# Two slots of scores and four banks of value sums in an attention stage whose ScalarE hardly rests

## The chip, the cores and the metric

The kernel runs on one core of one Trainium2 chip. The metric is the device time of one execution in microseconds (us); lower is better. A core has the matrix engine TensorE (PE), the vector engine VectorE (DVE), ScalarE (ACT), GpSimd (POOL) and the queue engine SyncE (SP). Each runs its own program in order, and they wait for one another through counting semaphores. Matmuls write to PSUM, which holds 8 banks of 512 fp32 values for each of its 128 partitions.

## The reference, cut to what matters

Input x is 2 sequences of 1024 tokens with 128 channels. Four layers follow one another, `x = x + layer(layernorm(x))`, in the order A (a gated recurrence), F, B (a Fourier layer), F. The change lies in layer F, which is run twice with the same weights:

```python
h = _rms(x, n1_w)
q = _rms(heads(wq), qn_w); k = _rms(heads(wk), kn_w); v = heads(wv)   # 16 heads of 8 channels
scores = einsum('bhqd,bhkd->bhqk', q, k) * HD ** (-0.5)
scores = where(causal, scores, -inf)
attn = softmax(scores)
ao = einsum('bhqk,bhkd->bhqd', attn, v) @ wo.T
x = x + ao                      # then a mixture of four small expert networks
```

The reference calls the layer with T = 1024 tokens and B = 2 sequences, so the attention is causal over 1024 x 1024 for 32 pairs of sequence and head.

## The kernel before, in words

Attention in `hybrid_kernel` is a list of units, `ATT` (L1129 to L1131). The outer index `it` is an item: one of the 2 sequences and one of 4 groups of four heads, 8 items in a layer. Inside an item the queries are taken in two chunks of 512 (`qc` 0 and 1), the keys in tiles of 128 (`kt` 0 to 3 for `qc` 0, and 0 to 7 for `qc` 1). On the diagonal the columns left of `c0` are skipped. A unit is one slot of scores and one exponential. Where c0 is 0 or 128, a key tile is two units of two heads each; where c0 is 256 or 384, one unit has all four heads. So an item has 20 units, here called u0 to u19:

- `qc` 0: u0, u1 (kt 0, 512 columns), u2, u3 (kt 1, 384 columns), u4 (kt 2, 256), u5 (kt 3, 128).
- `qc` 1: u6 to u15 (kt 0 to 4, two units each, 512 columns), u16, u17 (kt 5, 384), u18 (kt 6, 256), u19 (kt 7, 128).

In elements of a partition, an exponential is 1024 wide in fourteen units (512 columns by two heads, or 256 by four), 768 in u2, u3, u16 and u17, and 512 in u5 and u19. Sixteen items, or 320 units, are worked through in the whole kernel.

Four engines share the work of a unit u:

- PE in `f_tensor`, the loop of L1258: the scores S(u), matmuls of L1271 (bf16), into the slot `u % DEPTH` of two banks. Ahead of them stands `wait_ge(probs_ready, rep * NA + u + 1)` (L1265). ACT raises this semaphore by DEPTH at the start (L1390) and by one with every exponential, so S(u) waits for the exponential of unit u - DEPTH. Behind S(u) in the same loop, PE works on the unit w = u - 4 (`LAG`), if w ends a key tile: the value sums V(w), matmuls of L1289 (fp32), four heads beside one another in four strips of 32 rows of one bank. V(w) waits for the exponential of w (L1280), for its mask if it lies on the diagonal (L1282), and at kt 0 for `o_read` (L1284), that is, until DVE has read the sums that this bank held before.
- ACT in `f_scalar` (L1438 to L1445): the exponential X(u), from the slot into one of six buffers `PX` (PDEPTH).
- POOL in `f_gpsimd` (L1217 to L1224): the mask of the twelve units of an item that lie on the diagonal (u0 to u5, u14 to u19), a multiplication in PX. Ahead of u4 it also copies the values of the next item (L1211).
- DVE in `f_vector` (L1542 to L1561): when the last key tile of a chunk is summed, it reads the bank twice, with a shuffle (L1552) and, after a reciprocal (L1554), with a multiplication (L1556), which sets `o_read`; then it adds into `AO` (L1560).

The eight banks are split 6 to 2: slots of scores in banks 0 to 5, value sums in banks 6 and 7, one for each `qc`. What PE does in order around the change is thus ... S(15), V(11), S(16), S(17), V(13), S(18), S(19), V(15), then of the next item S(0), S(1), V(17), S(2), V(18), S(3), V(19), S(4), S(5), V(1), S(6), S(7), V(3), S(8), V(4), S(9), V(5), S(10), S(11), V(7) ... A V in the first half of this list is one of the item before.

After attention come the output projection and the experts, which use the banks anew; they wait for all of the above.

Of the kernel before, what the change touches and what calls it, by code (L numbers as in the profile page):

```python
# [27 lines left out]
CH = 512  # L28
# [64 lines left out]
def hybrid_kernel(nc, x, a_w, a_wab, a_small, a_conv, a_bog, a_bout, a_wout, b_w, b_dft, b_idft,  # L93
                  f_w, f_n, f_qk, f_mid, f_down, f_wo, f_rows, eye, causal, out):
    ctx = ExitStack()
    with ctx:
# [3 lines left out]
        def sb(name, shape, dt=F32, at=None, side=None):  # L100
            return (at or ctx).enter_context(nc.sbuf_tensor(name, shape, dt, side=side))
# [16 lines left out]
        PS = ctx.enter_context(nc.psum_tensor("PS", [P, 8, CH], F32))  # L118
# [85 lines left out]
        with ExitStack() as sw:  # L204
# [15 lines left out]
            VA = [sb(f"VA{i}", [P, TB, GH, 32], at=sw) for i in range(2)]  # L220
# [166 lines left out]
        def dve_norm(v, link, ans, eps, dst, rms_eps=None):  # L387

            v.tensor_scalar(stat[:], mv[:, :, 1], eps, None, ALU.add).then_inc(to_act, 1)  # L389
            ans.wait()  # L390
            link(v.reciprocal(rstd[:], stat[:]))
            scale = rstd
            if rms_eps is not None:

                link(v.tensor_tensor(var[:], mv[:, :, 1], rstd[:], ALU.mult))
                link(v.tensor_tensor(var[:], var[:], rstd[:], ALU.mult))
                v.tensor_scalar(stat[:], var[:], rms_eps, None, ALU.add).then_inc(to_act, 1)
                ans.wait()
                link(v.reciprocal(rrms[:], stat[:]))
                link(v.tensor_tensor(rrms[:], rrms[:], rstd[:], ALU.mult))  # L400
                scale = rrms
            for b in range(B):
                for t in range(b * TB, (b + 1) * TB):
                    last = center_and_scale(v, dst, t, scale)
                last.then_inc(normed, 1)
# [13 lines left out]
        def act_sqrt(act, ask, ap):  # L419
            ask.wait()  # L420
            act.activation(ap, ap, ACT.Sqrt).then_inc(to_dve, 1)  # L421
# [714 lines left out]
        NA_Q0 = len([a for a in ATT if a[0] == 0 and a[1] == 0])  # L1136
        TILE_END = [u for u in range(NA) if ATT[u][3][-1] == GH - 1]
        LAG = 4
        DEPTH = 3
        OBANKS = 2  # L1140
        SCORES_BANKS = 2 * DEPTH
        ROUTER_BANK = 5
        HT_BANKS = 4
# [46 lines left out]
        def f_gpsimd(pool, link, nth, rep):  # L1190
# [15 lines left out]
            def values(it):  # L1206
                b, g = divmod(it, NG)
                if it >= 2:
                    pool.wait_ge(probs_used, PDEPTH + (rep * B * NG + it - 1) * NA_B)
                src = QKV[:, b * TB:(b + 1) * TB, 2 * D + g * (GH * HD):2 * D + (g + 1) * (GH * HD)]  # L1210
                pool.tensor_copy(VA[it % 2][:, :, :, HD * g:HD * (g + 1)],  # L1211
                                 src.rearrange("p t (h d) -> p t h d", d=HD)).then_inc(v_ready, 1)
# [4 lines left out]
            for u in DIAG:  # L1217
                it, qc, kt, heads, c0 = ATT[u]
                if it >= 1 and it + 1 < B * NG and (qc, kt, heads[0]) == (0, 2, 0):
                    values(it + 1)  # L1220
                pool.wait_ge(probs_ready, DEPTH + rep * NA + u + 1)
                halves = len(heads) // 2
# [3 lines left out]
        def f_tensor(pe, banks, nth, rep):  # L1226
# [11 lines left out]
            for b in range(B):  # L1238
# [4 lines left out]
                for c in chunks:  # L1243
                    for n in range(2):
                        k = banks.take()
                        for i in range(TPC):
                            last = pe.transpose(PS[:, k, i * P:(i + 1) * P], QKS[:, c * TPC + i, n * D:(n + 1) * D],
                                                ident[:])
                        last.then_inc(psum_full, 1)
                pe.wait_ge(shifts_ready, rep * B + b + 1)  # L1250
                for c in chunks:
                    k = banks.take()
                    for i in range(TPC):
                        last = pe.transpose(PS[0:H, k, i * P:(i + 1) * P], qst2[:, c * TPC + i, 0:H], ident[:])
# [3 lines left out]
            for u in range(NA + LAG):  # L1258
                if u < NA:
                    it, qc, kt, heads, c0 = ATT[u]  # L1260
                    b = it % 2
                    if u % NA_B == 0:
                        pe.wait_ge(stack_loaded[b], 64 * (rep * NG + it // 2 + 1))
                        pe.wait_ge(v_ready, rep * B * NG + it + 1)
                    pe.wait_ge(probs_ready, rep * NA + u + 1)  # L1265
                    for two in range(0, len(heads), 2):
                        at = two // 2 * (CH // 2)
                        for side in range(2):
                            rows = slice(SIDE * side, SIDE * (side + 1))
                            pair = heads[two] // 2  # L1270
                            last = pe.matmul(PS[:, 2 * (u % DEPTH) + side, at:at + CH - c0],  # L1271
                                             KS[b][rows, pair, kt * P:(kt + 1) * P],
                                             QS[b][rows, pair, qc * CH + c0:(qc + 1) * CH], start=True, stop=True)
                    last.then_inc(scores_ready, 1)
                if u - LAG in TILE_END:
                    w = u - LAG
                    it, qc, kt, heads, c0 = ATT[w]
                    b = it % 2
                    units = GH // len(heads)
                    pe.wait_ge(probs_ready, DEPTH + rep * NA + w + 1)  # L1280
                    if w in DIAG:
                        pe.wait_ge(probs_masked, rep * len(DIAG) + DIAG_DONE[w])  # L1282
                    if kt == 0:
                        pe.wait_ge(o_read, (rep * B * NG + it) * 2 + qc + 1)  # L1284
                    for h in range(GH):
                        px = PX[(w - (units - 1) + h // len(heads)) % PDEPTH]
                        i = h % len(heads)
                        at = i // 2 * (CH // 2)
                        last = pe.matmul(PS[32 * h:32 * h + 32, SCORES_BANKS + qc, c0:CH], VA[b][:, kt, h, :],  # L1289
                                         px[:, i % 2, at:at + CH - c0], start=(kt == 0),  # L1290
                                         stop=(kt >= TPC * qc), skip_group_check=True)
                    last.then_inc(probs_used, units)

            for c in range(NCH):
                if c % (NCH // B) == 0:
                    pe.wait_ge(heads_added, (rep * B + c // (NCH // B) + 1) * (NG - 1) * 2)
                for i in range(TPC):
                    t = (c * TPC + i) * P
                    last = pe.matmul(PS[:, c, i * OUTC:(i + 1) * OUTC], AO[:, t:t + P], fwo[:], start=True, stop=True)
# [17 lines left out]
            for t in range(TILES):  # L1317
                last = pe.matmul(PS[:, ROUTER_BANK, t * E4:(t + 1) * E4], HT[:, t * P:(t + 1) * P],
                                 fw[:, F_GATE:F_GATE + E4], start=True, stop=True)
# [68 lines left out]
        def f_scalar(act, link, ask, reads, nth, rep):  # L1388
            if rep == 0:
                act.sem_inc(probs_ready, DEPTH)  # L1390
            act_sqrt(act, ask, stat[:])
# [46 lines left out]
            for u in range(NA):  # L1438
                heads, c0 = ATT[u][3:]
                halves = len(heads) // 2  # L1440
                tile = lambda t: t.rearrange("p k (n q) -> p k n q", n=halves)[:, :, :, 0:CH - c0]
                k = 2 * (u % DEPTH)
                act.wait_ge(scores_ready, rep * NA + u + 1)
# [31 lines left out]
        def f_vector(v, link, ans, nth, rep):  # L1475
            base = FIRST_RESULT[nth]
            v.wait_ge(x_ready, nth)
            if rep == 0:
                v.sem_inc(o_read, OBANKS)
            dve_norm(v, link, ans, LN_EPS, SQ, F_EPS)  # L1480
# [61 lines left out]
            for it in range(B * NG):  # L1542
                b, g = divmod(it, NG)
                for qc in range(2):
                    at = (rep * B * NG + it) * 2 + qc
                    o = PS[:, SCORES_BANKS + qc, :]
                    t = b * S + qc * CH
                    v.wait_ge(probs_used, PDEPTH + (rep * B * NG + it) * NA_B + (NA_Q0 if qc == 0 else NA_B))
                    v.wait_ge(o_read, OBANKS + at)
                    if added:  # L1550
                        v.wait_ge(heads_added, added)
                    v.stream_shuffle(DEN[:], o, [HD * (g + 1) % 32] * 32).then_inc(den_ready, 1)  # L1552
                    v.wait_ge(den_ready, 2 * at + 1)
                    v.reciprocal(DEN[:], DEN[:]).then_inc(den_ready, 1)  # L1554
                    v.wait_ge(den_ready, 2 * at + 2)
                    v.scalar_tensor_tensor(out=DEN[:] if g else AO[:, t:t + CH], in0=o, scalar=frows[:, g:g + 1],  # L1556
                                           in1=DEN[:], op0=ALU.mult, op1=ALU.mult).then_inc(o_read, 1)
                    if g:
                        v.wait_ge(o_read, OBANKS + at + 1)
                        v.tensor_tensor(AO[:, t:t + CH], AO[:, t:t + CH], DEN[:], ALU.add).then_inc(heads_added, 1)  # L1560
                        added += 1  # L1561
# [102 lines left out]
        @block.tensor  # L1664
        def _(pe):
            banks = Banks(pe)
            for n, layer in enumerate(LAYERS):
                if layer == "A":
                    a_tensor(pe, banks)
                elif layer == "B":  # L1670
                    b_tensor(pe, banks, n)
                else:
                    f_tensor(pe, banks, n, LAYERS[:n].count("F"))
# [105 lines left out]
```

## Time and profile before

| | us |
|---|---|
| median of 3 runs | 1206.76 |
| lowest and highest run | 1203.33, 1211.42 |
| the profiled execution, its own time | 1207.07 |
| its span in the profile | 1205.2 |

The profile holds one execution. Times are us from the start of its span, unless they are marked ns. PE is the matmuls and PEld the loads of weights beside them. A row of a timeline gives start, length, engine, line, operation and shapes, how many instructions are merged in it, and in brackets how long the engine sat idle before it and what ended that. Instructions of a pipelined engine overlap, so the length of one is more than the distance between two. A wait for several semaphores is put down to the engine that came last by the profile, and this may be the wrong one. PEclk is the granted TensorE clock as a share of 2.4 GHz.

### The profile page before, as it was taken

The numbers are of one execution on the slowest core, as the hardware profiler recorded it, in microseconds if no ns is written. First come the engines' busy times: TensorE is split into PE (matmuls) and PEld (weight loads), VectorE is DVE, ScalarE is ACT, GpSimd is POOL, SyncE is SP. The second block draws the span as 40 slices with busy tenths as digits, with TensorE's granted clock in tenths as the row PEclk, the third lists the DMA queues.
The fourth block names the chain that finished last, engine by engine and source line by source line (L and its number), as shares of the span: only waits on it lengthen the run. The fifth ranks groups of instructions, "written<-read, shape, count | busy, mean of one in ns | idle before, by whom it ended". The sixth has DMA issues, their size and how long they took to land.

```text
span 1205.2 us, 11485 instructions
## 1 busy us (share of the span) xinstructions
PE 674.5 (56%) x4014; PEld 333.1 (28%) x4014; DVE 867.5 (72%) x1306; ACT 506.5 (42%) x752; POOL 403.4 (33%) x334
## 2 busy tenths in 40 slices
PE   4990000040004004479899799963264799978997
PEld 2450000040004003222222556631243122225655
DVE  6899999999999995856657733269959557667212
ACT  3423000122220001579999322243034899973321
POOL 1250847600006602226765000006802566650000
PEclk9985555555555556779999799987565899997999
DMA  2250006172000020223310000000003242100001
GB/s 92 70 140 1 1 0 140 35 168 63 13 14 14 0 35 0 84 75 116 97 33 22 1 1 1 1 0 1 0 0 115 63 142 54 54 1 1 1 1 35
DMA packets 30258, 50.71 MB, mean 42 GB/s; under 512 B 4472, under 2 KB 14328, under 8 KB 29176
## 3 DMA queue, kind: packets, MB, share of 16 engines
q1 hardware_dynamic: 29432, 49.32, 15.2%
q10 hardware_dynamic: 768, 0.66, 0.3%
q8 instruction: 32, 0.52, 0.2%
q14 instruction: 26, 0.21, 0.1%
HBM read 20.98 MB, written 16.92 MB: 31 GB/s over the span
## 4 chain that ended last, share of the span: by engine, by line
DVE 47%; PE 23%; ACT 16%; issue 10%; POOL 1%; DMA 1%; ACTq 1%; POOLq 0%; SPq 0%; DVEq 0%
ACT PX L1445 10%; PE PS L1330 6%; PE PS L1308 5%; PE PS L1350 4%; PE PS L1289 3%; DVE D L813 2%; DVE S L817 2%; DVE P L814 2%; DVE PS L871 2%; DVE PRD L870 2%; DVE mag L1031 2%; DVE PA L772 2%; ACT P L688 2%; DVE RO L837 2%; DVE RP L832 2%
## 5 line engine op out<-in xcount | busy, mean ns | idle before, releaser
L1445 ACT ACTIVATE PX<-PS 128x1024 f32<-128x1024 f32 (+1 forms) x320 | 268.1, 1016 | 12.1 <-PE PS L1271 12.1
L1224 POOL TENSOR_TENSOR PX<-PX,maskf 128x256 f32<-128x256 f32 (+1 forms) x192 | 173.4, 931 | 125.0 <-ACT PX L1445 124.5
L1289 PE MATMUL PS<-PX,VA 128*32 128x512 f32 (+3 forms) x1536 | 166.2, 503 | 22.3 <-POOL PX L1224 14.5
L1617 DVE SCALAR_TENSOR_TENSOR X<-PS,wts,X 128x96 f32<-128x96 f32 x128 | 38.4, 315 | 118.2 <-PE PS L1350 103.9
L1271 PE MATMUL PS<-QS,KS 64*128 64x512 bf16 (+3 forms) x768 | 107.8, 339 | 16.7 <-issue 11.4
L1554 DVE RECIPROCAL DEN<-DEN 128x512 f32<-128x512 f32 x32 | 107.3, 3353 | 1.1
L580 PE MATMUL PS<-ones,HT 64*128 64x1 f32 x64 | 13.0, 348 | 152.0 <-ACT HT L672 152.0
L947 POOL TENSOR_TENSOR PRQ<-PA,LQK 128x2048 f32<-128x2048 f32 (+15 forms) x16 | 39.9, 2520 | 151.8 <-DMA WS<-S 138.6
L1552 DVE LOAD_MASK_SELECT DEN<-PS x32 | 0.4, 14 | 107.2 <-PE PS L1289 93.5
L591 PE MATMUL PS<-awout,V 64*128 64x128 f32 x64 | 13.3, 422 | 110.5 <-DVE vss L820 110.5
L1308 PE MATMUL PS<-HT,fw 128*128 128x512 f32 x144 | 71.2, 638 | 3.9 <-DVE HG L1584 2.6
L1271 PEld LDWEIGHTS PS<-QS,KS 64*128 64x128 bf16 x768 | 30.3, 94 | 155.5 <-ACT PX L1445 111.3
L1085 POOL TENSOR_TENSOR KV<-QF 65x1024 f32<-65x1024 f32 x3 | 9.1, 3038 | 159.8 <-DVE QF L1035 157.5
L935 POOL TENSOR_TENSOR PRP<-LQK,XL 128x2048 f32<-128x2048 f32 (+15 forms) x16 | 39.6, 2488 | 56.8 <-DVE LQK L758 41.4
L688 ACT ACTIVATE P<-S,AC 128x16 f32<-128x16 f32 x64 | 20.5, 321 | 89.4 <-DVE S L817 89.4
L580 PEld LDWEIGHTS PS<-ones,HT 64*128 64x128 f32 x64 | 12.9, 329 | 152.3 <-issue 152.3
L1289 PEld LDWEIGHTS PS<-PX,VA 128*32 128x32 f32 x1536 | 33.0, 108 | 74.7 <-ACT PX L1445 38.3
L421 ACT ACTIVATE stat<-stat 128x16 f32<-128x16 f32 (+1 forms) x10 | 2.1, 213 | 107.6 <-DVE stat L389 81.6
L600 PE MATMUL PS<-awout,RT 128*128 128x128 f32 x32 | 6.2, 382 | 71.0 <-DMA RT<-RO 71.0
L591 PEld LDWEIGHTS PS<-awout,V 64*128 64x128 f32 x64 | 13.0, 329 | 110.6 <-issue 110.6
L560 PE MATMUL PS<-HT,CWT 128*128 128x512 f32 (+3 forms) x96 | 41.4, 593 | 0.0
L982 PE MATMUL PS<-bidft,YF 65*128 65x128 f32 x64 | 15.1, 431 | 43.8 <-POOL YF L1102 40.8
(264 smaller groups left out, 1649.5 us busy)
## 6 DMA issues: line engine op xcount, KB each, us to landing
QS<-qs_d SPq DMA_DIRECT2D x32, 196.0 KB
qs_d<-QP SPq DMA_DIRECT2D x24, 256.0 KB, 3.9
ks_d<-QP SPq DMA_DIRECT2D x24, 256.0 KB, 4.0
KS<-ks_d SPq DMA_DIRECT2D x32, 192.0 KB
K<-LQK SPq DMA_DIRECT2D x16, 256.0 KB
W<-WS SPq DMA_DIRECT2D x16, 256.0 KB, 4.1
qkv_d<-CY SPq DMA_DIRECT2D x3, 1024.0 KB, 3.9
LQK<-qkv_d SPq DMA_DIRECT2D x8, 256.0 KB, 4.9
```

The source lines that it names most:

```text
L560: last = pe.matmul(PS[:, k, skip:CH], CWT[:, 4 * n + j, :], HT[:, t + skip - back:t + CH - back], start=(j == 3), stop=True, skip_group_ch ...
L688: act.activation(P2[:, :, :, C], S2[:, n], ACT.Copy, scale=AC2[:, g, c:c + 1]).then_inc(s_slot, 1)
L935: pool.tensor_tensor(pp, qn[:, :, s:C, :], bcast(kb[:, :, s, :], 2, n), ALU.mult).then_inc(prod_ready, 1)
L947: pool.tensor_tensor(pq, bcast(PA[:, :, t, 0:t + 1], 2, HD), dj[:, :, :, 0:t + 1], ALU.mult).then_inc(rprod_ready, 1)
L1224: pool.tensor_tensor(block, block, bcast(maskf[:], 1, 2 * halves), ALU.mult).then_inc(probs_masked, 1)
L1271: last = pe.matmul(PS[:, 2 * (u % DEPTH) + side, at:at + CH - c0], KS[b][rows, pair, kt * P:(kt + 1) * P], QS[b][rows, pair, qc * CH + c0: ...
L1289: last = pe.matmul(PS[32 * h:32 * h + 32, SCORES_BANKS + qc, c0:CH], VA[b][:, kt, h, :], px[:, i % 2, at:at + CH - c0], start=(kt == 0), s ...
L1308: last = pe.matmul(PS[:, bank + m, :], fw[:, col + m * P:col + (m + 1) * P], rhs(c), start=True, stop=True)
L1330: last = pe.matmul(PS[:, bank + m, :], fmid[:, w + k, m * P:(m + 1) * P], h, start=(k == 0), stop=(k == len(parts) - 1))
L1350: last = pe.matmul(PS[:, 6 + t % 2, j * OUTC:(j + 1) * OUTC], h[:, m, t * P:(t + 1) * P], fdown[:, e, m, :], start=(m == 0), stop=(m == 1))
L1445: act.activation(tile(PX[u % PDEPTH][:]), tile(PS[:, k:k + 2, :]), ACT.Exp).then_inc(probs_ready, 1)
L1554: v.reciprocal(DEN[:], DEN[:]).then_inc(den_ready, 1)
```

## The change

DEPTH goes from 3 to 2 and OBANKS from 2 to 4. The slots of scores are then banks 0 to 3 (`SCORES_BANKS = 2 * DEPTH`), and S(u) waits for X(u - 2). The value sums have banks 4 to 7, one for each `qc` and each parity of the item, and `o_read` starts at 4, so that V at kt 0 waits for DVE's reading of the item before the last. Order, shapes and number of all instructions stay.

```diff
-        DEPTH = 3
-        OBANKS = 2
+        DEPTH = 2
+        OBANKS = 4
...
-                        last = pe.matmul(PS[32 * h:32 * h + 32, SCORES_BANKS + qc, c0:CH], VA[b][:, kt, h, :],
+                        last = pe.matmul(PS[32 * h:32 * h + 32, SCORES_BANKS + 2 * b + qc, c0:CH], VA[b][:, kt, h, :],
...
-                    o = PS[:, SCORES_BANKS + qc, :]
+                    o = PS[:, SCORES_BANKS + 2 * (it % 2) + qc, :]
```

## Rows read from the trace of the kernel before

**Rows 1.** The page: span, and the span in 40 slices.
```profile
span 1205.2 us, 11485 instructions
...
ACT 3423000122220001579999322243034899973321
...
PEclk9985555555555556779999799987565899997999
```

**Rows 2.** The page: costliest groups of the attention stage.
```profile
L1445 ACT ACTIVATE PX<-PS 128x1024 f32<-128x1024 f32 (+1 forms) x320 | 268.1, 1016 | 12.1 <-PE PS L1271 12.1
...
L1289 PE MATMUL PS<-PX,VA 128*32 128x512 f32 (+3 forms) x1536 | 166.2, 503 | 22.3 <-POOL PX L1224 14.5
...
L1271 PE MATMUL PS<-QS,KS 64*128 64x512 bf16 (+3 forms) x768 | 107.8, 339 | 16.7 <-issue 11.4
```

**Rows 3.** Timeline of ACT from u6 of one item to u6 of the next.
```profile
581.71 16.73 ACT L1445 ACTIVATE PX<-PS 128x1024 f32<-128x1024 f32 x20 [0.36 <-PE PS L1271]
598.80 16.73 ACT L1445 ACTIVATE PX<-PS 128x1024 f32<-128x1024 f32 x20 [0.35 <-PE PS L1271]
```

**Rows 4.** Busy time by stretches: us, PE, PEld, DVE, ACT, POOL, PEclk, DMA share, GB/s.
```profile
598.80:615.89 17.09, 15.54 (x146) 3.90 (x144) 10.41 (x10) 16.73 (x21) 10.95 (x14) 1.00 0.17 46
```

**Rows 5.** Timeline of ACT, short windows: X(14), X(15), X(16), X(17), X(19), X(6).
```profile
588.96 1.10 ACT L1445 ACTIVATE PX<-PS 128x1024 f32<-128x1024 f32 x1
589.87 1.12 ACT L1445 ACTIVATE PX<-PS 128x1024 f32<-128x1024 f32 x1
590.77 0.92 ACT L1445 ACTIVATE PX<-PS 128x768 f32<-128x768 f32 x1
...
591.46 1.85 ACT L1445 ACTIVATE PX<-PS 128x768 f32<-128x768 f32 x2
...
593.06 1.66 ACT L1445 ACTIVATE PX<-PS 128x512 f32<-128x512 f32 x2
...
598.80 1.03 ACT L1445 ACTIVATE PX<-PS 128x1024 f32<-128x1024 f32 x1 [0.35 <-PE PS L1271]
```

**Rows 6.** Timeline of PE: S(15), V(11), S(16), S(17), V(13), S(18) and S(19).
```profile
588.29 0.39 PE L1271 MATMUL PS<-QS,KS 64*128 64x512 bf16 x2
...
588.61 1.07 PE L1289 MATMUL PS<-PX,VA 128*32 128x512 f32 x8
...
589.61 0.34 PE L1271 MATMUL PS<-QS,KS 64*128 64x384 bf16 x2
...
590.13 0.34 PE L1271 MATMUL PS<-QS,KS 64*128 64x384 bf16 x2 [0.18 <-ACT PX L1445]
590.39 1.07 PE L1289 MATMUL PS<-PX,VA 128*32 128x512 f32 x8
591.39 0.64 PE L1271 MATMUL PS<-QS,KS 64*128 64x256 bf16 x8
```

**Rows 7.** Timeline of PE: V(1), then S(6) and S(7).
```profile
597.37 1.06 PE L1289 MATMUL PS<-PX,VA 128*32 128x512 f32 x8 [0.47 <-ACT PX L1445]
598.37 0.61 PE L1271 MATMUL PS<-QS,KS 64*128 64x512 bf16 x4
```

**Rows 8.** Timeline of POOL: masks of u14; u15 to u3; then u18 alone; u1, u2.
```profile
590.15 0.73 POOL L1224 TENSOR_TENSOR PX<-PX,maskf 128x256 f32<-128x256 f32 x1 [5.77 <-ACT PX L1445]
591.07 7.58 POOL L1224 TENSOR_TENSOR PX<-PX,maskf 128x256 f32<-128x256 f32 x9 [0.19 <-ACT PX L1445]
...
593.39 1.28 POOL L1224 TENSOR_TENSOR PX<-PX,maskf 128x512 f32<-128x512 f32 x1
...
596.54 1.42 POOL L1224 TENSOR_TENSOR PX<-PX,maskf 128x256 f32<-128x256 f32 x2
```

**Rows 9.** Timeline of DVE: bank of `qc` 0 set free, then that of `qc` 1.
```profile
589.40 0.75 DVE L1556 SCALAR_TENSOR_TENSOR DEN<-PS,frows,DEN 128x512 f32<-128x512 f32 x1
...
600.69 0.75 DVE L1556 SCALAR_TENSOR_TENSOR DEN<-PS,frows,DEN 128x512 f32<-128x512 f32 x1
```

**Rows 10.** Timeline of PE: the V(7) that takes the bank of `qc` 1 next.
```profile
602.50 1.06 PE L1289 MATMUL PS<-PX,VA 128*32 128x512 f32 x8
```

**Rows 11.** Busy time by stretches as in Rows 4, and PE's first V.
```profile
524.00:530.00 6.00, 5.12 (x28) 0.85 (x24) 1.22 (x5) 4.98 (x7) 4.28 (x6) 0.50 0.17 57
...
527.26 1.93 PE L1289 MATMUL PS<-PX,VA 128*32 128x512 f32 x8
```

## The prediction

> **What bounds the kernel now.** I read the page first. ACT stands at its highest in slices 18 to 22 and again from 31 on, with the clock at 9 tenths nearly throughout [rows 1]; these are the two attention stages. By the groups of the page, the exponentials are busy for 268.1 us and leave ACT idle for only 12.1 us, always waiting for scores, while on PE the value sums and the scores are busy for 166.2 and 107.8 us [rows 2]. So ACT sets the pace and PE is close behind. The timeline of ACT shows how regular this is: blocks of 20 exponentials, 16.73 us long, and one gap of 0.35 or 0.36 us ahead of X(6), so an item takes 17.09 us [rows 3]. There are 14 such distances, 7 in each stage. In one of them PE is busy for 15.54 us, ACT for 16.73, POOL for 10.95 and DVE for 10.41, at a granted clock of 1.00, the upper of the two levels, 2.4 GHz [rows 4].
>
> So the change takes a slot from the hand-over between PE and ACT, which decides, and gives banks to the one between PE and DVE. It adds and removes no instruction; only waits move.
>
> **The added value banks: 0 us.** What they could remove is a wait of V(1) or V(7) for DVE. PE does stand idle for 0.47 us ahead of V(1), put down to ACT [rows 7]. But V(1) waits for three things. Its exponential ended long before. The bank of `qc` 0 was set free at 589.40 + 0.75 = 590.15 [rows 9], 7.2 us before V(1) starts. The mask of u1 starts at 596.54; two masks are 1.42 us long, so the next follows about 0.7 later, at 597.23 [rows 8], and V(1) starts at 597.37, 0.14 after that. POOL is the real releaser, and that stays. The other bank is free at 600.69 + 0.75 = 601.44 [rows 9], and V(7) comes at 602.50 [rows 10]: 1.06 us to spare. Two banks for sums were enough.
>
> **The missing slot, its step times.** Let E be the end of an exponential.
> - X: a 1024 wide exponential follows the last by 0.90 us (588.96 to 589.87 to 590.77), a 768 wide one takes 0.69 (590.77 to 591.46). In a queue one lasts 1.10 to 1.12 us from start to end; after a gap, 1.03 [rows 5].
> - E to S: X(14) ends at 588.96 + 1.10 = 590.06 [rows 5], and S(17), which waits for it, starts at 590.13 [rows 6]: 0.07.
> - S to X: S(6) starts at 598.37 [rows 7], X(6) at 598.80 [rows 5]: 0.43.
> - S to V behind it: 588.29 to 588.61 is 0.32 with 512 columns, 590.13 to 590.39 is 0.26 with 384. A V of 512 columns holds PE for 1.00 us (588.61 to 589.61, 590.39 to 591.39) [rows 6].
>
> **In the run of full pairs (u6 to u15).** With two slots S(b), of the second unit of a pair, waits for the second exponential of the pair before. Behind it stands V, and behind V the S of the next pair. The loop is E to S 0.07, S to V 0.32, V 1.00, S to X 0.43, then two exponentials to the end of the second, 0.90 + 1.03: together 3.75 us, over two pairs, for which ACT needs 4 x 0.90 = 3.60 to 3.62. So the loop is just too long, by 0.13 to 0.15 in two pairs. Walked through one item from X(10), the delays come to 0.12 ahead of X(12), 0.01 at X(14), 0.06 at X(16); I take 0.19. The lower end is 0 (the exponential's own spread of 1.03 to 1.12 us covers it), the upper 0.08 in each of 5 pairs, 0.4.
>
> **At the narrowing diagonal (u16 to u19).** Here is the large term. S(17) now waits for X(15) in place of X(14): one exponential, 0.90 us, later. V(13) with its 1.00 us stands behind S(17), and S(18) behind V(13). Before, S(18) started at 591.39 [rows 6], so X(18) could have started at 591.82 and did at 591.46 + 0.69 = 592.15 [rows 5]: slack 0.33. The new delay of X(18) is thus 0.90 - 0.33 = 0.57, with the 0.06 just counted in it, so about 0.5 of its own; 0.33 of this shows as idle time of ACT, the rest is the overlap of two exponentials that goes. The two 768 wide exponentials are too short to hide a V of 1.00 us. X(0) loses 0.08 more in the same way, as S(0) waits behind V(15).
>
> **Given back at X(6)?** The gap of 0.36 us is POOL's: masks without a break from 590.15 to 591.07 + 7.58 = 598.65, and on [rows 8]. If POOL's work kept its time, a late ACT would be absorbed there. But the mask of u18 must wait for the late X(18), and before, POOL took it at 593.39 [rows 8], only 0.1 us after X(18) ended (592.15 and some 1.1); so POOL is pushed back 0.45 to 0.5, V(1) with it, and the gap stays at about 0.34. I give back 0.07.
>
> Sum for an item, with 0.05 of rounding taken off: 0.19 + 0.50 + 0.08 - 0.07 - 0.05 = 0.65; the walk through all 20 units gives 0.64, or 17.73 us in place of 17.09. Times 14: 9.0 us. The ends of the two stages hold one more item each, of which the first third runs at a clock of 0.50, where V takes 1.93 us [rows 11] and PE is late in any case; the passage u16 to u19 is still there. I take 0.5 us each, 1.0. The total is 10.0 us, on the profiled execution's 1207.07 (span 1205.2 and 1.9 around it): **1217.1 us**. The median shown lies 0.3 below that execution.
>
> **Rivals.**
> - *The loss is hidden* (chance 0.13). The mean slack before X and the gap ahead of X(6) take it up, and POOL catches up. For it: the gap is 0.36 us in every item, 5.8 us in 16. Against it: POOL's masks run without a break. It gives 0.1 to 0.2 us an item: 1209.
> - *Every V of 512 columns tells* (0.22). If E to S or S to V is 0.1 us longer where PE really waits, each of the 7 such V of an item adds 0.08, so 0.6 more an item and 10 us in all: 1227. For it: PE would wait for ACT at nearly every unit, and with one exponential in hand nothing evens out a hiccup. Against it: the 0.07 is from a real wait.
> - *Two slots do and four banks pay* (0.04), the side of a gain. If the 0.47 us ahead of V(1) were the wait for DVE after all, the extra banks would end it, and with it the gap ahead of X(6), 16 x 0.36 = 5.8 us; at most all 12.1 us of ACT's idle time [rows 2]: 1195.0. It decides only if the bank, not the mask, comes last at V(1), and rows 8 and 9 put the bank 7 us earlier. The Trainium skill ("Perfetto Trace Analysis", Matmuls) advises to rotate independent matmul groups through different banks, so that emptying one overlaps the next group; for the sums the trace shows no wait that this would end, and for the scores the change does the reverse.
> - *The clock falls* (0.04). PE's rests grow from 9% of an item (1 - 15.54 / 17.09) to 12% in many small pieces. If that took the clock to its lower level, 1.2 GHz, for a quarter of the time, PE, with V at 1.93 us in place of 1.06 [rows 10 and 11], would need some 1.8 x 15.5 = 28 us for an item in those parts, or 2.6 us more on the mean of 16: 1258. Against it: it stays at 1.00 in rows 4 with a rest every other unit. The Trainium skill ("TensorE: Matmul & The Clock Gate", A second HAM failure mode: psum-queue depth-cycling) tells of a kernel whose clock swung because PE idled briefly between groups as it cycled through banks; no row here shows it in the attention stages.
>
> **How the numbers follow.** My forecast has 0.57, and by itself it spans 1213 to 1221. A measurement tells about 1% from no change, 12.1 us here; 1219.1 is the border, so the forecast is mostly within it, with 0.15 beyond, and the two slower rivals add 0.26. That makes slower 0.40, faster 0.03 (the third rival falls just on the border), the same 0.57. The range reaches down to the hidden case and up beyond the second rival: 1209 to 1229.
>
> **What would show it.** In the changed profile: blocks of ACT about 17.7 us apart in place of 17.09; two gaps of about 0.3 us in an item, one ahead of X(18), one ahead of X(6), and ACT's idle time before exponentials near 17 us in place of 12.1 (16 times 0.33 more; the rest of the loss is overlap of two exponentials that goes, which no gap shows); S(17) 0.07 us after the end of X(15), no longer X(14); V(1) still 0.14 us after POOL's mask of u1; DVE's times unchanged; the clock at 1.00. It would be wrong if the distance stayed at 17.1 (hidden), if gaps stood before every other exponential and it were above 18.2 (second rival), or if time changed outside the two attention stages.

## The result, and the profile after

The changed kernel takes 1218.95 us (median of 6 runs, 1217.42 to 1223.04) beside 1206.40 us for the kernel before (6 runs, 1203.33 to 1211.65). The ratio is 1.0105, with a 95% interval of 1.0081 to 1.0129: slower by about 1%. The forecast was 1217.1 us in a range of 1209 to 1229. The profiled execution took 1219.92 us, 12.85 more than that of before.

The page of the changed kernel, the lines that answer to [rows 1, 2]:

```profile
span 1218.1 us, 11485 instructions
...
PEclk9985555555555556689999799986575899997999
...
L1445 ACT ACTIVATE PX<-PS 128x1024 f32<-128x1024 f32 (+1 forms) x320 | 273.0, 947 | 17.6 <-PE PS L1271 16.5
...
L1289 PE MATMUL PS<-PX,VA 128*32 128x512 f32 (+3 forms) x1536 | 165.6, 504 | 6.1 <-POOL PX L1224 6.1
L1271 PE MATMUL PS<-QS,KS 64*128 64x512 bf16 (+3 forms) x768 | 115.3, 339 | 36.5 <-ACT PX L1445 20.3
```

The matmuls are the same in number and mean length. What changed is who waits: PE is now idle for 36.5 us just ahead of scores in place of 16.7, and for 6.1 us ahead of value sums in place of 22.3. ACT's idle time before exponentials went from 12.1 to 17.6 us. The mean exponential became *shorter*, 947 ns in place of 1016. That is no gain: in a queue, the start of an exponential is recorded while the one before still runs (by 0.19 us at X(15) of [rows 5], 589.87 against 590.06), so its record is longer; with two slots fewer of them queue. The busy time of the group grew from 268.1 to 273.0 us.

ACT's timeline, one item from X(6) on (answers to [rows 3]), and the stretch of that item by engine (answers to [rows 4]):

```profile
602.17 10.78 ACT L1445 ACTIVATE PX<-PS 128x1024 f32<-128x1024 f32 x12 [0.29 <-PE PS L1271]
613.27 6.35 ACT L1445 ACTIVATE PX<-PS 128x1024 f32<-128x1024 f32 x8 [0.33 <-PE PS L1271]
619.92 10.78 ACT L1445 ACTIVATE PX<-PS 128x1024 f32<-128x1024 f32 x12 [0.29 <-PE PS L1271]
```

```profile
602.17:619.92 17.75, 16.00 (x146) 4.01 (x144) 10.38 (x10) 17.04 (x21) 10.96 (x14) 1.00 0.18 42
```

The distance of items is 17.75 us in place of 17.09, and there are two gaps in place of one: ahead of X(18), the thirteenth exponential after the first gap, and ahead of X(6). The clock stays at 1.00.

PE at the narrowing diagonal of the same item, S(17), V(13), then S(18) and S(19) (answers to [rows 6]):

```profile
611.57 0.34 PE L1271 MATMUL PS<-QS,KS 64*128 64x384 bf16 x2 [0.18 <-ACT PX L1445]
611.84 1.06 PE L1289 MATMUL PS<-PX,VA 128*32 128x512 f32 x8
612.84 0.50 PE L1271 MATMUL PS<-QS,KS 64*128 64x256 bf16 x8
```

From S(17) to V(13) it is 0.27, from V(13) to S(18) 1.00, and from S(18) at 612.84 to X(18) at 613.27 it is 0.43, as before the change. S(17) now starts 0.05 us after X(15) has ended (a start of 610.50 and 1.02), where it started 0.07 after X(14).

### The profile page after: what moved, and what is told of

It is laid out like the page before. It is cut to its first block, busy times and chain, and to the rows that moved or that the text cites. A ratio compares the mean times of both kernels' runs of the same rounds, so it can differ in the third digit from the quotient of the medians.

```text
span 1218.1 us, 11485 instructions
## 1 busy us (share of the span) xinstructions
PE 683.6 (56%) x4014; PEld 334.5 (27%) x4014; DVE 865.2 (71%) x1306; ACT 511.4 (42%) x752; POOL 404.8 (33%) x334
## 4 chain that ended last, share of the span: by engine, by line
DVE 47%; PE 28%; ACT 14%; issue 9%; DMA 1%; POOL 1%; ACTq 1%; POOLq 0%; SPq 0%; DVEq 0%
ACT PX L1445 8%; PE PS L1330 6%; PE PS L1289 5%; PE PS L1308 5%; PE PS L1350 4%; PE PS L1271 3%; DVE D L813 2%; DVE S L817 2%; DVE P L814 2%; DVE PS L871 2%; DVE PRD L870 2%; DVE mag L1031 2%; DVE PA L772 2%; ACT P L688 2%; DVE RO L837 2%
## 5 line engine op out<-in xcount | busy, mean ns | idle before, releaser
L1445 ACT ACTIVATE PX<-PS 128x1024 f32<-128x1024 f32 (+1 forms) x320 | 273.0, 947 | 17.6 <-PE PS L1271 16.5
L1271 PE MATMUL PS<-QS,KS 64*128 64x512 bf16 (+3 forms) x768 | 115.3, 339 | 36.5 <-ACT PX L1445 20.3
L1271 PEld LDWEIGHTS PS<-QS,KS 64*128 64x128 bf16 x768 | 33.0, 93 | 191.6 <-ACT PX L1445 164.2
```

The lines of the kernel that those rows point to most:

```text
L1445: act.activation(tile(PX[u % PDEPTH][:]), tile(PS[:, k:k + 2, :]), ACT.Exp).then_inc(probs_ready, 1)
```

## Experiments

The ten edits below are small. Where a distance is given, it is that of items in the steady part of a profile; 17.09 is before, 17.75 after. Each ratio is to runs of the kernel before that were made beside the experiment; their medians are 1207.71 us (experiments 1 to 3), 1208.77 (5 and 6) and 1208.97 (4).

**1. The wait alone.** Three slots and two banks of sums stay as in the kernel before; S(u) waits one exponential longer.

```diff
-                    pe.wait_ge(probs_ready, rep * NA + u + 1)
+                    pe.wait_ge(probs_ready, rep * NA + u + 1 + (1))
```

> Before, with three slots and two banks of sums, but every S(u) waits for X(u-2) in place of X(u-3): only the wait of the change, none of its banks. Slot theory: the wait is everything, so the time of the changed kernel, 1217 to 1220 us, distance of items 17.74 us. Rival, bank placement: if the new layout of banks costs or gives something by itself, the time differs from that by over 2 us.

Measured: 1219.71 us, ratio 1.0092 (1.0079 to 1.0106), and in ACT's timeline:

```profile
604.54 10.78 ACT L1445 ACTIVATE PX<-PS 128x1024 f32<-128x1024 f32 x12 [0.29 <-PE PS L1271]
615.64 6.35 ACT L1445 ACTIVATE PX<-PS 128x1024 f32<-128x1024 f32 x8 [0.33 <-PE PS L1271]
622.28 10.78 ACT L1445 ACTIVATE PX<-PS 128x1024 f32<-128x1024 f32 x12 [0.29 <-PE PS L1271]
```

Distance 17.74, the same two gaps. The wait is the whole effect; where the tiles lie in PSUM gives and costs nothing that these numbers can tell, 0.01 us in an item.

**2. Two slots, two banks of sums.**

```diff
-        DEPTH = 3
+        DEPTH = 2
         OBANKS = 2
```

> Two slots of scores and only two banks for sums (two PSUM banks unused). Slot theory: the third and fourth bank of sums give nothing, so the time is that of the changed kernel, 1217 to 1220 us, distance 17.74. Rival (the added banks pay for part of the lost slot): slower than the changed kernel by 2 us or more, with idle time ahead of V(1) or V(7).

Measured: 1219.53 us, ratio 1.0094 (1.0082 to 1.0106).

```profile
599.66 10.79 ACT L1445 ACTIVATE PX<-PS 128x1024 f32<-128x1024 f32 x12 [0.29 <-PE PS L1271]
610.77 6.36 ACT L1445 ACTIVATE PX<-PS 128x1024 f32<-128x1024 f32 x8 [0.32 <-PE PS L1271]
617.42 10.79 ACT L1445 ACTIVATE PX<-PS 128x1024 f32<-128x1024 f32 x12 [0.29 <-PE PS L1271]
```

Distance 17.76. Two banks may be left unused and nothing changes beyond 0.01 us in an item: with two slots the added banks of sums are worth nothing.

**3. The wait in one part only.** The edit of experiment 1 on the kernel before, once in u6 to u15 (full pairs), once in all others.

```diff
+ ... + (1 if 6 <= u % NA_B <= 15 else 0))     # w2, pairs
+ ... + (0 if 6 <= u % NA_B <= 15 else 1))     # w3, diagonal
```

> As before, but only u6 to u15, the full pairs, wait for X(u-2). Slot theory: in these the loop is too long by little. X(14) ends some 0.08 us later counted from X(6), and from there POOL's masks lead to the next X(6), so the distance of items grows by 0.08 us, from 17.09 to 17.17: some 1.2 us in all, 1208. Rival (every V of 512 columns tells): each of five pairs loses, 0.4 us or more in an item, 1213 or more.

> As before, but only u16 to u19 and u0 to u5, the passage over the diagonal, wait for X(u-2). Slot theory: here is the large term. The distance grows by 0.5 to 0.58 us to about 17.6, with about 1.2 us at the start and 0.5 at the end of each stage: 1216 to 1218. Rival (loss spread evenly over V's): half of the whole loss, 1212 to 1213.

Measured: pairs 1212.77 us, ratio 1.0032 (1.0019 to 1.0045); diagonal 1218.56 us, ratio 1.0092 (1.0078 to 1.0107). ACT's timeline, first pairs, then diagonal:

```profile
604.34 16.94 ACT L1445 ACTIVATE PX<-PS 128x1024 f32<-128x1024 f32 x20 [0.34 <-PE PS L1271]
621.62 16.94 ACT L1445 ACTIVATE PX<-PS 128x1024 f32<-128x1024 f32 x20 [0.34 <-PE PS L1271]
```

```profile
601.31 10.69 ACT L1445 ACTIVATE PX<-PS 128x1024 f32<-128x1024 f32 x12 [0.29 <-PE PS L1271]
612.34 6.36 ACT L1445 ACTIVATE PX<-PS 128x1024 f32<-128x1024 f32 x8 [0.34 <-PE PS L1271]
618.99 10.69 ACT L1445 ACTIVATE PX<-PS 128x1024 f32<-128x1024 f32 x12 [0.29 <-PE PS L1271]
```

The diagonal alone brings 17.68, 0.59 more than before: the large term is where it was put. The pairs alone bring 17.28, 0.19 more, and not the 0.08 that this run's expectation had. That expectation let POOL's masks lead from X(14) to the next X(6). They do not: what leads there is the mask of u18, and it waits for X(18). The next item of the kernel before, POOL:

```profile
608.85 1.44 POOL L1224 TENSOR_TENSOR PX<-PX,maskf 128x256 f32<-128x256 f32 x2
610.47 1.28 POOL L1224 TENSOR_TENSOR PX<-PX,maskf 128x512 f32<-128x512 f32 x1 [0.18 <-ACT PX L1445]
```

POOL waits 0.18 us for X(18) there. In the item of [rows 8] it does not pause, since there the mask of u17 ends just when that of u18 can start, at 593.39. But in all 16 items the mask of u18 starts 0.08 us after the end of X(18), and the next X(6) starts 5.41 to 5.45 us after the start of that mask. So whatever delays X(18) delays the next X(6) in full, and the gap ahead of X(6) absorbs none of it.

And the pairs do delay X(18). PE in w2, S(15), V(11), S(16) with S(17), V(13), and S(18) with S(19):

```profile
611.91 0.39 PE L1271 MATMUL PS<-QS,KS 64*128 64x512 bf16 x2 [0.20 <-ACT PX L1445]
612.23 1.06 PE L1289 MATMUL PS<-PX,VA 128*32 128x512 f32 x8
613.23 0.50 PE L1271 MATMUL PS<-QS,KS 64*128 64x384 bf16 x4
613.66 1.07 PE L1289 MATMUL PS<-PX,VA 128*32 128x512 f32 x8
614.66 0.50 PE L1271 MATMUL PS<-QS,KS 64*128 64x256 bf16 x8
```

S(15) is held until X(13) has ended. From there PE works without a rest to S(18), and X(18) starts 0.43 us after that, at 615.09. Counted from X(6), X(15) ends only 0.09 us later than before (9.36 in place of 9.27) and X(18) 0.18 later; the second half of the delay arises in this chain.

Also 0.19 and 0.59 make 0.78, more than the 0.66 of both together. In the whole change S(17) waits for X(15) anyway, so this chain adds nothing, and the delayed pairs cost only 0.07 us at X(15): its end comes 9.35 us after X(6) in the changed kernel and 9.28 in w3. The late exponentials no longer queue and last 1.02 us in place of 1.12, so they hand on later starts almost without later ends.

**4. The diagonal split once more.**

```diff
+ ... + (1 if u % NA_B >= 16 else 0))          # w4, u16 to u19
+ ... + (1 if u % NA_B <= 5 else 0))           # w5, u0 to u5
```

> As before, but only u16 to u19 wait for X(u-2). Theory: S(17), V(13), S(18) make X(18) late by 0.59 us, and POOL, whose run of masks begins anew with that of u18, is late by 0.46; V(1) follows the mask of u1 and X(6) follows V(1): distance 17.55 to 17.6, no extra gap at the start of a stage (0.78 us ahead of the first X(6), as before). 7 to 8 us in all: 1215. Rival (the early units carry a good part of the loss): distance under 17.4, under 1213.

> As before, but only u0 to u5 wait for X(u-2). Theory: S(5) then waits for X(3) and V(1) stands behind it 0.1 us later than behind POOL's mask, so the distance grows by 0.1 us to 17.19; and the start of each stage, where the clock is low and four scores are wanted at once, loses 0.6 to 0.7 us. 3 us in all: 1210 to 1211. Rival (the start costs nothing, as the prediction had it): under 1.5 us in all, gap ahead of the first X(6) 0.78 us as before.

Measured: w4 1216.33 us, ratio 1.0061 (1.0040 to 1.0081); w5 1211.01 us, ratio 1.0016 (0.9998 to 1.0034), which by itself is not clear of no change. Their timelines are. ACT in w4, then in w5 with the start of a stage:

```profile
600.12 10.68 ACT L1445 ACTIVATE PX<-PS 128x1024 f32<-128x1024 f32 x12 [0.33 <-PE PS L1271]
611.15 6.18 ACT L1445 ACTIVATE PX<-PS 128x1024 f32<-128x1024 f32 x8 [0.34 <-PE PS L1271]
617.67 10.68 ACT L1445 ACTIVATE PX<-PS 128x1024 f32<-128x1024 f32 x12 [0.34 <-PE PS L1271]
```

```profile
530.80 1.94 ACT L1445 ACTIVATE PX<-PS 128x1024 f32<-128x1024 f32 x2 [1.38 <-PE PS L1271]
...
600.21 16.92 ACT L1445 ACTIVATE PX<-PS 128x1024 f32<-128x1024 f32 x20 [0.29 <-PE PS L1271]
617.43 16.92 ACT L1445 ACTIVATE PX<-PS 128x1024 f32<-128x1024 f32 x20 [0.29 <-PE PS L1271]
```

u16 to u19 bring 17.55, 0.45 to 0.46 us of the 0.66; u0 to u5 bring 17.22, 0.13. Together this is the 0.59 of w3. And u0 to u5 carry a cost that the prediction had set at nothing: the gap ahead of a stage's first X(6) is 1.38 us, as in the changed kernel, against 0.78 before and in w2 and w4.

**5. Is it V(13)?** In the changed kernel V(13), then V(13) and V(15), are cut to 32 of their 512 columns, so that one or two key tiles of each item are almost left out of the result.

```diff
+                    end = c0 + 32 if w % NA_B in (13,) else CH      # v1;  v2: (13, 15)
...
-                        last = pe.matmul(PS[32 * h:32 * h + 32, SCORES_BANKS + 2 * b + qc, c0:CH], VA[b][:, kt, h, :],
-                                         px[:, i % 2, at:at + CH - c0], start=(kt == 0),
+                        last = pe.matmul(PS[32 * h:32 * h + 32, SCORES_BANKS + 2 * b + qc, c0:end], VA[b][:, kt, h, :],
+                                         px[:, i % 2, at:at + end - c0], start=(kt == 0),
```

> The changed kernel with the value sums V(13) cut to 32 of their 512 columns, so one key tile of each item is nearly left out of the result and PE is free about 0.9 us earlier there. Theory of the loop: the gap ahead of X(18) goes, but S(19) then waits for X(17) with V(15) behind it, and X(0) is late instead; walked through, an item gets shorter by only 0.20 us, to 17.54, some 3 us in all: 1216. Rival, as the prediction put it (the whole term of 0.5 us hangs on V(13) behind S(17)): 17.2 us for an item, 1211 to 1212.

> The changed kernel with V(13) and V(15) both cut to 32 of 512 columns. Theory of the loop: with both out of the way X(0) is on time but for 0.15 us; an item takes 17.74 - 0.5 = 17.2 us, 1211 to 1212. What is left is the pairs and the gap ahead of X(6). Rival (the two waits for exponentials alone cost the time, whatever stands behind them): little changes, 1216 or more.

Measured: v1 1215.90 us, ratio 1.0069 (1.0044 to 1.0093); v2 1213.78 us, ratio 1.0039 (1.0021 to 1.0058). ACT, v1 and then v2:

```profile
598.16 12.18 ACT L1446 ACTIVATE PX<-PS 128x1024 f32<-128x1024 f32 x14 [0.29 <-PE PS L1271]
610.63 4.75 ACT L1446 ACTIVATE PX<-PS 128x1024 f32<-128x1024 f32 x6 [0.29 <-PE PS L1271]
615.68 12.18 ACT L1446 ACTIVATE PX<-PS 128x1024 f32<-128x1024 f32 x14 [0.29 <-PE PS L1271]
```

```profile
580.43 17.02 ACT L1446 ACTIVATE PX<-PS 128x1024 f32<-128x1024 f32 x20 [0.29 <-PE PS L1271]
597.74 17.02 ACT L1446 ACTIVATE PX<-PS 128x1024 f32<-128x1024 f32 x20 [0.29 <-PE PS L1271]
```

Without V(13) the block is 14 long: the gap has moved by two units to X(0), and an item takes 17.52 us. The cut V(13) lasts 0.27 us in place of 1.06, at the very place of the stall, and this gives 0.23. With V(15) gone as well it is 17.31, 0.1 more than expected, and the gap at X(18) or X(0) is gone from the steady items (0.09 us are left ahead of X(0), too few for the view to show). So the term of 0.5 us does not hang on V(13) alone; two waits stand one behind the other, each long enough to hold ACT up, and the first hides the second.

Two of the 14 distances of v2 are 18.36 and 18.32 us. There the granted clock fell, which it did in no other profile here between the first item of a stage and its end. In the first case PE was busy for 14.34 of the 17.00 us before:

```profile
610.81:627.81 17.00, 14.34 (x147) 3.96 (x144) 10.36 (x9) 16.62 (x21) 10.81 (x13) 1.00 0.18 50
627.81:631.22 3.41, 3.41 (x28) 0.61 (x20) 0.00 (x0) 2.58 (x4) 3.41 (x5) 0.50 0.00 0
```

The two stretches at the lower level cost this execution 2.1 us. So of the time of v2 a part may be the clock's; no trace shows whether its other runs had them.

**6. Who sets the gap ahead of X(6)?** The mask of u18 goes from POOL to DVE, in the kernel before (d1) and in the changed one (d2). DVE does it between its work for the two chunks of an item, where it idled. The rest of the edit, which counts the masks of POOL and of DVE apart, is left out here.

```diff
+        ON_DVE = [u for u in range(NA) if u % NA_B in (18,)]
+        ON_POOL = [u for u in DIAG if u not in ON_DVE]
...
-            for u in DIAG:
+            for u in ON_POOL:
...
+                    if qc:
+                        for u in ON_DVE:
+                            if ATT[u][0] == it:
+                                v.wait_ge(probs_ready, DEPTH + rep * NA + u + 1)
...
+                                v.tensor_tensor(block, block, bcast(maskf[:], 1, 2 * (len(ATT[u][3]) // 2)), ALU.mult).then_inc(dve_masked, 1)
```

> Before (three slots), with the mask of u18 taken from POOL to DVE, which is idle then. Theory: with three slots POOL's masks set the gap of 0.36 us ahead of X(6). POOL is relieved of 1.25 us, the gap goes, and an item takes about 16.75 us: 5 us less, 1201 to 1202. Rival (PE or the exponentials set it): unchanged at 17.09, 1206.

> The changed kernel (two slots) with the mask of u18 on DVE. Theory: with two slots V(1) stands behind S(5), which waits for X(3), and POOL is 0.1 us ahead of that; so relief for POOL gives nothing, 17.74 us an item, 1218 to 1219. Rival, as the prediction put it (POOL pushed back is what keeps the gap ahead of X(6)): the gap of 0.3 us goes, 17.4 us an item, 1213 to 1214.

Measured: d1 1198.83 us, ratio 0.9928 (0.9900 to 0.9956), **faster than both kernels** and by more than expected; d2 1218.26 us, ratio 1.0092 (1.0069 to 1.0115), as without the edit. ACT in d1 and the busy time of about one item there, then ACT in d2:

```profile
534.21 126.78 ACT L1451 ACTIVATE PX<-PS 128x1024 f32<-128x1024 f32 x152 [0.47 <-PE PS L1275]
```

```profile
600.00:616.70 16.70, 15.89 (x146) 3.88 (x144) 11.17 (x11) 16.70 (x22) 9.81 (x13) 1.00 0.17 44
```

```profile
604.51 10.78 ACT L1451 ACTIVATE PX<-PS 128x1024 f32<-128x1024 f32 x12 [0.29 <-PE PS L1275]
615.61 6.35 ACT L1451 ACTIVATE PX<-PS 128x1024 f32<-128x1024 f32 x8 [0.33 <-PE PS L1275]
622.25 10.78 ACT L1451 ACTIVATE PX<-PS 128x1024 f32<-128x1024 f32 x12 [0.29 <-PE PS L1275]
```

With three slots POOL was the cause: relieve it, and 152 exponentials follow one another with no gap that the view shows. The steady distances are 16.52 to 16.73 us, 16.63 on the mean, so 0.46 less than before. The end of each stage, from the last X(6) on, is 0.55 us shorter too, which the expectation had left out; from the first X(0) to the last V(19) the two stages are 7.1 us shorter together. With two slots the same relief gives nothing. POOL and PE in the changed kernel (the experiment aside) tell why: masks of u0 and u1, then S(5) and V(1):

```profile
616.84 1.42 POOL L1224 TENSOR_TENSOR PX<-PX,maskf 128x256 f32<-128x256 f32 x2
```

```profile
618.27 0.28 PE L1271 MATMUL PS<-QS,KS 64*128 64x128 bf16 x4 [0.31 <-ACT PX L1445]
618.49 1.07 PE L1289 MATMUL PS<-PX,VA 128*32 128x512 f32 x8
```

The mask of u1 is done at 618.26. In the kernel before, V(1) starts 0.10 us after the end of this mask, so here it could at 618.36. But S(5) stands ahead of it, waits for X(3), and holds it until 618.49, 0.13 later. This is the 0.13 us that u0 to u5 bring by themselves (w5). In d2 the mask is done 0.87 us ahead of V(1), and V(1) still follows S(5) by 0.22. The gap is about as long as before (0.29 and 0.36 us) and has another owner.

## Why the prediction was right, and where not

- **The banks of sums, 0 us.** Right: experiments 1 and 2.
- **The distance of items, 17.73.** Measured 17.75. The two gaps came where they were put, ahead of X(18) and X(6), at 0.33 and 0.29 us where 0.33 and 0.34 were named, and ACT's idle time is 17.6 us for the 17 foretold. The mechanism, S(17) waiting for X(15) with V(13) behind it, holds by w4.
- **Its terms.** Here the sum is better than its parts, and that is in part luck. The pairs' 0.19 agrees in size with w2, but half of that arises on the way to X(18) and not at X(12) to X(16), and in the whole change the pairs hand on only 0.07. The diagonal's 0.50 and 0.08, less 0.07, measured 0.59 alone (w3). The errors have opposite signs, and 0.05 of rounding was taken off besides. As the traces show it, the 0.66 is two delays: X(18) ends 12.13 us after X(6) in place of 11.60, and V(1), behind S(5), adds 0.13. In place of this second one the prediction had 0.08 at X(0) and 0.07 given back at X(6).
- **V(13) behind S(17) as the place.** Right for the gap that is seen, wrong as the price of it: without V(13) only 0.23 us comes back (v1), since V(15) behind S(19) is next.
- **"POOL is pushed back, V(1) with it, and the gap stays".** The gap stayed for another reason: V(1) now follows S(5) by 0.22 us and the end of its mask by 0.23, in place of 0.10 before, and relief for POOL gives nothing (d2). That POOL's masks ran "without a break" from u14 was misread too: the mask of u18 starts by the end of X(18) in every item, so POOL had no work queued behind X(18) that could take up its delay.
- **The ends of the stages, 1.0 us.** This is the mis-sized term. From the last X(6) to the start of the last V(19) it is 14.85 us in place of 14.33, 0.5 in each stage, as reckoned. But the start of a stage was put at nothing, with the words "PE is late in any case", and that was wrong: at the low clock the first two slots fill later, and S(2) and S(3) wait for the first exponentials. From the first X(0) to the first X(6) it is 6.24 us in place of 5.53, 0.7 in each stage (and 6.24 in w5 too). That is 2.5 us in all.
- **Fourteen distances, 9.0 us.** Between those points the two stages grew by 9.0 us (3.9 and 5.1), and this agreement hides two disturbances. Twelve of the distances grew by 0.65 or 0.66 us. The first distance of a stage depends on the clock as well. Two microseconds from the first X(6) on, for the first and second stage of the kernel before, then of the changed one:

```profile
529.77:531.77 2.00, 2.00 (x12) 0.31 (x10) 0.00 (x0) 1.94 (x2) 1.30 (x2) 0.50 0.00 0
945.24:947.24 2.00, 2.00 (x22) 0.48 (x20) 0.00 (x0) 2.00 (x3) 1.29 (x2) 0.97 0.00 0
531.18:533.18 2.00, 2.00 (x21) 0.42 (x20) 0.00 (x0) 2.00 (x3) 0.75 (x1) 0.94 0.00 0
952.60:954.60 2.00, 2.00 (x12) 0.30 (x10) 0.00 (x0) 1.94 (x2) 0.70 (x1) 0.50 0.00 0
```

  The distances that begin there are 17.76, 17.09, 17.75 and 18.24 us: where the clock was still at its lower level, 0.66 and 0.50 more than the steady ones. It is so in all twelve profiles. In the 13 stages in which the clock rose by 1.2 us after the first X(6), the first distance is at most 0.10 us longer than the later ones; in the 11 in which it rose 2.1 to 3.0 us after, it is 0.42 to 0.87 longer. Each kernel had one of either kind here, so the two nearly cancel; the change itself brings 14 times 0.66, or 9.2.
- **The rest.** The distances and the ends make 11.5 of the 12.85. Nearly all of the rest is the start of the two stages, 0.70 and 0.77 us later against the work ahead of them. By the code S(0) waits there for loads, and the idle time ahead of the first exponential lies anywhere between 0.5 and 3.3 us in these profiles, even among kernels with the same start. Whether any of it belongs to the change stays open.
- **The border.** The prediction gave 0.57 to "the same" and 0.40 to "slower", with the border at 1%. The ratio of 1.0105 lies on that border and its interval across it, so the result does not favour either.
- **The rivals.** Hidden loss: out, by the distance. Every V telling: out, as the pairs give 0.19 and no gap before X(12) or X(14). Four banks that pay: out, by experiment 2. The clock: 1.00 in the steady stretch of both. PE's rests did grow, from 1.55 us of 17.09 to 1.75 of 17.75, which is 10% and not the 12% reckoned, but the swing that the Trainium skill ("TensorE: Matmul & The Clock Gate", A second HAM failure mode: psum-queue depth-cycling) tells of did not come in the steady items of this kernel. It was not out of reach, as v2 shows.

## What to carry to other kernels

Where two engines hand tiles to each other through slots and one of them does other work in the same queue, take the loop through a slot: wait, that engine's step, the other work behind it, the hand-over, and the consumer's steps; compare it with the consumer's pace over as many units as there are slots, and do so at the units where the consumer is fastest (here the narrow exponentials), for there the slots ran out first. A resource without a wait of its own in the trace, such as the two banks of sums, gives nothing when it is doubled. And before work is taken from an engine to close a gap, ask what is 0.1 us behind it: the same relief of POOL gave 0.7% with three slots and nothing with two.

## What the runs showed of the hardware that was not expected

A queued exponential of 1024 elements lasts longer in the record than a lone one: 1.10 to 1.19 us in the kernel before (1.19 at X(1), 611.53) and up to 1.42 in d1, where ACT has no gaps, against 1.02. Yet they follow one another by 0.90 to 0.92 us in either case. So a shorter mean can go with a slower kernel, and idle time is not the whole loss: it grew by 5.5 us where the kernel lost 12.5.

One kernel can meet the rise of the clock at the start of a stage early or late, and the first item is up to 0.9 us longer for it. Two profiles that are compared by their spans alone carry this difference along; steady distances do not.
